# Graph convolution with two feature sets on one Trainium2 core: one more short turn at the start, sums on other tiles, later loads of x, and halves in the middle items

## The chip, the cores and the metric

The kernel runs on one core of one Trainium2 chip. The metric is the device time of one execution in microseconds. Before the change it is 392.65 us, the median of three runs (392.62 to 392.72).

## The reference

Both layers share the matrix, so the kernel treats x and spatial_x as one matrix of 256 columns:

```python
N, IN_DIM, HID = 4096, 128, 128
def _gcn_layer(x, adj, W, b):
    d_inv_sqrt = (jnp.sum(adj, axis=1) + 1e-09) ** (-0.5)
    msg = d_inv_sqrt[:, None] * adj * d_inv_sqrt[None, :] @ x
    return jax.nn.relu(msg @ W + b)
H_f = _gcn_layer(x, adj, W_f, b_f)
H_s = _gcn_layer(spatial_x, adj, W_s, b_s)
attn = jax.nn.sigmoid(jnp.concatenate([H_f, H_s], axis=1) @ W_att + b_att)
out = _layernorm(x + attn * H_f + (1.0 - attn) * H_s)
```

adj is 4096 x 4096 in float32, 64 MiB, and is read twice: once transposed for the product, once in natural order for the row sums.

## The kernel before, in words

The product A @ Y, where Y = D x (D is the row's inverse root), is cut into j-tiles (t, 32 tiles of 128 columns of adj) and row groups (g, 8 groups of 512 rows). A block is one t and one g, 128 x 512 numbers of the transposed matrix. Four blocks make an item, one transfer of 1 MiB, and `plan` lists the 64 items. A run is a row group with a list of tiles that are summed in one pair of PSUM banks (`pair`, four of them) before VectorE adds the pair into `acc` (an evacuation, two halves, `evacuate`). A turn is the set of four runs that take the pairs in their order; the groups 0 to 3 and the groups 4, 6, 5, 7 take turns. At the start of the program D is known for few tiles, so turns are short there; later a turn has four tiles: two old ones, whose blocks stand two by two in `column` items, and two fresh ones in `spread` items. The last eight tiles (item 48, FINAL, and on) go group by group.

Each item goes through the engines thus:

- SyncE issues the transfers in program order: `parts[k]` (pieces of natural rows for the row sums, up to 1 MiB), x, then item k into one of three `raw` buffers. It waits for VectorE's `low` of item k-3, and for GpSimd's sums of it.
- ScalarE makes Ah, `raw` rounded to fp32r (`high`), and sums the parts (`row_sum`, with an accumulator); `y_high` makes Yh.
- VectorE makes Al = raw - Ah (`low`), Yl (`y_low`), and evacuates. The order of these is written out in its loop over k.
- TensorE runs three products for each block and half of Y: Yh Ah, Yl Ah, Yh Al; an item has 24 matmuls of 512 columns. Up to item 21, `first_block` takes the first block in an order that needs Al and Yl late, and the two halves of Y end together.
- GpSimd makes D from the row sums (`degree`), and adds the blocks of row groups 6 and 7 for the j-tiles in SUMMED into S (`sum_block`), so that the last rows' sums need not be read in full. `collect`, on TensorE after item 42, turns S into eight columns; it waits for all sums and for the last evacuation of pair 3.

`pieces(k)` says in how many parts Ah and Al are made: blocks (0), (1), (2, 3) up to item 13, two halves up to item 21, and one piece after that. One constant, HALVED = 22, sets where the pieces end, where `sweeps` groups two blocks of one run, and where VectorE's order changes.

## Time and profile before

| what | value |
|---|---|
| median of the runs | 392.65 us |
| the profiled execution, its own time | 393.04 us |
| its span in the trace | 391.2 us |
| TensorE busy | 378.3 us, 97% |
| VectorE busy | 303.2 us, 77% |
| ScalarE busy | 285.6 us, 73% |
| GpSimd busy | 155.3 us, 40% |
| granted TensorE clock, mean | 0.994 of full |
| HBM read | 128.32 MB |

The span is the time between the first and the last record; the 1.8 us around it belong to the execution's own time. Busy time of TensorE is modelled from pipelined matmuls and overlaps, so the starts of its weight loads (PEld) are the better measure of its pace. A row of the timeline gives start and length, and in brackets how long the engine stood idle ahead of it and who released it. Two rows of a kind that follow each other are merged (x2).

### The profile page before, as it was taken

The page shows a single profiled execution, that of the slowest core. Times are in us where ns is not written, and L with a number is a line of the kernel's source. Part 1 is how long each engine was busy: PE and PEld are TensorE (multiplying, and loading weights), DVE is VectorE, ACT ScalarE, POOL GpSimd, SP SyncE. Part 2 cuts the span into 40 slices and gives each one's busy share as a digit, 9 for nine tenths or more (in the row PEclk, how much of TensorE's full clock was granted, in tenths as well). Part 3 has the DMA queues.
Part 4 walks back from the last instruction along what each step waited for, and adds up shares of the span by engine and source line. Part 5 has one row for each costly group of instructions (what it writes and reads, how often), then busy time and mean ns, then how long its engine had stood idle before and what let it go on. Part 6 is the DMA issues. An engine that isn't in the chain of part 4 may idle for free. (4 is left out here: it accounts for less than half of the span.)

```text
span 391.2 us, 5501 instructions
## 1 busy us (share of the span) xinstructions
PE 378.3 (97%) x1778; PEld 314.0 (80%) x1778; DVE 303.2 (77%) x443; ACT 285.6 (73%) x381; POOL 155.3 (40%) x204
## 2 busy tenths in 40 slices
PE   7889999999999999999999999999999999999992
PEld 7667778788888888788888888888788888888992
DVE  2789997999578975769578583928976796889795
ACT  3668788888877887878878887778742666687556
POOL 2332611571066402670058220010100417877795
PEclk9999999999999999999999999999999999999997
DMA  8999999999999999999999999999775534445002
GB/s 268 423 417 424 420 412 421 423 419 418 421 416 421 423 418 420 421 420 422 418 423 420 424 414 423 413 390 415 232 281 208 213 108 160 164 157 168 4 25 81
DMA packets 24556, 130.77 MB, mean 334 GB/s; under 512 B 2640, under 2 KB 7632, under 8 KB 10448
## 3 DMA queue, kind: packets, MB, share of 16 engines
q1 hardware_dynamic: 24528, 130.43, 83.2%
q8 instruction: 14, 0.23, 0.2%
q14 instruction: 14, 0.11, 0.1%
HBM read 128.32 MB, written 2.10 MB: 333 GB/s over the span
## 5 line engine op out<-in xcount | busy, mean ns | idle before, releaser
L533 DVE TENSOR_TENSOR Al<-raw,Ah 128x2048 fp32r<-128x2048 f32 (+2 forms) x101 | 162.0, 1620 | 40.3 <-ACT Ah L721 40.2
L408 PE MATMUL sums<-Ah,Yh 128*128 128x512 f32 (+1 forms) x484 | 186.9, 386 | 1.3 <-DVE Al L533 1.3
L409 PE MATMUL sums<-Ah,Yl 128*128 128x512 f32 (+1 forms) x484 | 185.1, 382 | 0.0
L410 PE MATMUL sums<-Al,Yh 128*128 128x512 f32 (+1 forms) x484 | 185.0, 382 | 0.0
L721 ACT ACTIVATE Ah<-raw 128x2048 fp32r<-128x2048 f32 (+2 forms) x101 | 127.1, 1283 | 48.9 <-DMA raw<-in_At 29.9
L731 ACT ACTIVATE nat<-nat 128x2048 f32<-128x2048 f32 (+1 forms) x54 | 100.1, 1855 | 20.0 <-DMA nat<-in_adj 19.3
L408 PEld LDWEIGHTS sums<-Ah,Yh 128*128 128x128 f32 x484 | 91.0, 188 | 22.5 <-DVE Al L533 4.8
L410 PEld LDWEIGHTS sums<-Al,Yh 128*128 128x128 f32 x484 | 91.0, 188 | 17.9
L409 PEld LDWEIGHTS sums<-Ah,Yl 128*128 128x128 f32 x484 | 91.0, 188 | 17.1
L553 DVE TENSOR_TENSOR acc<-sums,acc 128x512 f32<-128x512 f32 (+1 forms) x122 | 76.8, 673 | 28.8 <-PE sums L410 25.2
L871 POOL TENSOR_TENSOR S<-S,raw 128x512 f32<-128x512 f32 x40 | 62.4, 1559 | 32.2 <-DMA raw<-in_At 29.2
L829 POOL TENSOR_SCALAR dg<-rs 128x1 f32<-128x1 f32 x23 | 13.9, 603 | 112.4 <-ACT nat L731 112.3
L877 POOL TENSOR_TENSOR fin<-fin 128x128 f32<-128x128 f32 x31 | 15.2, 491 | 31.3 <-ACT fin L755 31.2
L878 POOL TENSOR_TENSOR xs<-xs,fin 128x128 f32<-128x128 f32 x31 | 22.2, 715 | 0.0
L764 ACT ACTIVATE fin<-xs,less 128x128 f32<-128x128 f32 x30 | 11.7, 390 | 14.1 <-POOL less L883 14.1
L542 DVE SCALAR_TENSOR_TENSOR Yl<-xs,D,Yh 128x256 fp32r<-128x256 f32 x32 | 20.8, 664 | 0.1
L748 ACT ACTIVATE Yh<-xs,D 128x256 fp32r<-128x256 f32 x32 | 15.4, 496 | 4.7 <-POOL D L832 2.4
L597 DVE SCALAR_TENSOR_TENSOR xs<-fin,att,xs 128x128 f32<-128x128 f32 x30 | 12.0, 414 | 7.8 <-POOL xs L878 7.6
L755 ACT ACTIVATE fin<-nat 128x256 f32<-128x256 f32 x32 | 11.8, 410 | 8.1 <-DVE nat L567 8.0
L441 PEld LDWEIGHTS sums<-Wfs,acc 128*128 128x128 f32 x128 | 15.6, 191 | 1.0 <-DVE acc L553 0.5
L441 PE MATMUL sums<-Wfs,acc 128*128 128x128 f32 x128 | 16.3, 276 | 0.1
L832 POOL TENSOR_TENSOR D<-dg,mhalf 128x1 f32<-128x1 f32 x23 | 15.0, 652 | 1.9
(56 smaller groups left out, 201.2 us busy)
## 6 DMA issues: line engine op xcount, KB each, us to landing
raw<-in_At SPq DMA_DIRECT2D x63, 1024.0 KB, 9.8
nat<-in_adj SPq DMA_DIRECT2D x47, 1024.0 KB, 12.0
nat<-in_adj SPq DMA_DIRECT2D x8, 768.0 KB, 9.6
xs<-in_xs SPq DMA_DIRECT2D x5, 512.0 KB, 11.1
out<-xs SPq DMA_DIRECT2D x15, 128.0 KB, 1.8
xs<-in_xs SPq DMA_DIRECT2D x5, 256.0 KB, 11.5
nat<-in_adj SPq DMA_DIRECT2D x2, 512.0 KB, 6.6
raw<-in_At SPq DMA_DIRECT2D x2, 512.0 KB, 8.5
```

The costliest lines, as they stand in the source:

```text
L408: pe.matmul(to, Yh[:, t % YRING, hs], high, start=first, stop=False)
L409: pe.matmul(to, Yl[:, t % YRING, hs], high, start=False, stop=False)
L410: mm = pe.matmul(to, Yh[:, t % YRING, hs], low, start=False, stop=last)
L441: return pe.matmul(sums[:, 3, bank, c + half * H:c + (half + 1) * H], acc[:, r // GT, half, q * P:(q + 1) * P], Wfs[:, half * H:(half + 1) ...
L533: dve.tensor_tensor(Al[:, k % SPLITS, a * IB:b * IB], raw[:, k % RAWS, a * IB:b * IB], Ah[:, k % SPLITS, a * IB:b * IB], ALU.subtract).the ...
L542: dve.scalar_tensor_tensor(out=Yl[:, r % YRING, :], in0=xs[:, r, :], scalar=D[:, r:r + 1], in1=Yh[:, r % YRING, :].bitcast(F32), op0=ALU.mult,
L553: dve.tensor_tensor(acc[:, g, half, a:b], sums[:, pair, half, 0:b - a], acc[:, g, half, a:b], ALU.add).then_inc(evac_ok, 1)
L721: act.activation(Ah[:, k % SPLITS, a * IB:b * IB], raw[:, k % RAWS, a * IB:b * IB], ACT.Copy).then_inc(high_ok, b - a)
L731: act.activation(nat[:, n % NATS, 0:width], nat[:, n % NATS, 0:width], ACT.Copy, accum_out=rs[:, r, h:h + 1]).then_inc(rs_act, 1)
L748: act.activation(Yh[:, r % YRING, :], xs[:, r, :], ACT.Copy, scale=D[:, r:r + 1]).then_inc(Yh_ok, 1)
L871: pool.tensor_tensor(S[:, g, :], S[:, g, :], raw[:, k % RAWS, j * IB:(j + 1) * IB], ALU.add).then_inc(block_sum_ok, 1)
L878: pool.tensor_tensor(xs[:, r, 0:F], xs[:, r, 0:F], f[:, H_S], ALU.add).then_inc(res_ok, 1)
```

## The change

- `plan` has one more short turn: tiles [3, 4], [4, 5] and [5, 6, 7] in place of [3, 4, 5]; the longer turns begin with tiles 6 and 7, and the sets of row groups swap.
- GpSimd sums tiles 2 to 21 in place of 0 to 19. The rest of each of the last rows is then two stretches of columns, and its load two transfers.
- Parts 10 and 11 go from item 9 to item 10, 12 and 13 one item later each.
- x of four tiles (`X_AFTER`) is issued one item ahead of its use, not four.
- HALVED becomes two constants: BY_BLOCK = 22, as before, for the order of blocks and of VectorE, and IN_PARTS = 50 for `pieces` and `first_block`, so items 22 to 49 come in halves.
- At items 47 and 48 VectorE's evacuations and Yl stand in another order, and the run of item 45 in pair 3 (LATE) is evacuated last of these.

```diff
-HALVED = 22
+BY_BLOCK = 22
+IN_PARTS = 50
...
-    for n, tiles in enumerate([[0], [0, 1], [1, 2], [2, 3], [3, 4, 5]]):
+    for n, tiles in enumerate([[0], [0, 1], [1, 2], [2, 3], [3, 4], [4, 5], [5, 6, 7]]):
         spread(add_runs(sets[n % 2], tiles, range(4)), tiles)
-    for n in range(3, FRONT // 2):
+    for n in range(4, FRONT // 2):
         old, fresh = [2 * n - 2, 2 * n - 1], [2 * n, 2 * n + 1]
-        new = add_runs(sets[n % 2], old + fresh, range(4))
+        new = add_runs(sets[(n + 1) % 2], old + fresh, range(4))
...
-    evac_order = sorted(range(len(runs)), key=lambda e: done_no[e, 0])
+    LATE = next(e for e in range(len(runs)) if end_item[e] == FINAL - 3 and runs[e][2] == 3)
+    evac_order = sorted(set(range(len(runs))) - {LATE}, key=lambda e: done_no[e, 0])
+    evac_order.insert(1 + max(evac_order.index(e) for e in evac_order if end_item[e] == FINAL - 1), LATE)
...
-    SUMMED = range(5 * GT)
-    PLAIN_FROM = len(SUMMED) * P
+    SUMMED = range(2, 22)
+    PLAIN = [(0, SUMMED[0] * P), ((SUMMED[-1] + 1) * P, N)]
+    PLAIN_COLS = sum(b - a for a, b in PLAIN)
...
-    parts[4], parts[6], parts[8], parts[9] = [4, 5], [6, 7], [8, 9], [10, 11]
-    for n in range(12, 30):
+    parts[4], parts[6], parts[8], parts[10] = [4, 5], [6, 7], [8, 9], [10, 11]
+    parts[11], parts[12], parts[13] = [12], [13], [14, 15]
+    for n in range(16, 30):
         parts[n - 2].append(n)
...
-    X_AFTER = {y_position(m * GT) - 4: m for m in range(3, G)}
+    X_AFTER = {y_position(m * GT) - 1: m for m in range(3, G)}
...
-            return [(0, 2), (2, GT)] if k < HALVED else [(0, GT)]
+            return [(0, 2), (2, GT)] if k < IN_PARTS else [(0, GT)]
...
-                    in_first = k < HALVED and j == 0
+                    in_first = k < IN_PARTS and j == 0
...
-                        if k in (FINAL - 1, FINAL):
-                            evacuate_new(ending[:1])
-                        for r in y_at[k]:
+                        if k == FINAL:
+                            evacuate_new(ended)
+                        if k != FINAL - 1:
+                            for r in y_at[k]:
+                                y_low(r)
+                    elif k == FINAL - 1:
+                        evacuate_new(ending[:1])
+                        for r in y_at[k][:2]:
+                            y_low(r)
+                    elif k == FINAL:
+                        for r in y_at[k - 1][2:]:
                             y_low(r)
...
-                if k < HALVED or k in (FINAL - 1, FINAL):
+                if k < BY_BLOCK:
                     evacuate_new(ending)
+                if k == FINAL:
+                    evacuate_new(ending + [LATE])
```

VectorE, items 8 to 10 before. Al is `low`, Yl `y_low`, acc an evacuation (one row for each half of a run), the first four rows are item 8, the next four item 9:

```order
L533 TENSOR_TENSOR Al<-raw,Ah 128x512
L542 SCALAR_TENSOR_TENSOR Yl<-xs,D,Yh 128x256
L533 TENSOR_TENSOR Al<-raw,Ah 128x512
L533 TENSOR_TENSOR Al<-raw,Ah 128x1024
L533 TENSOR_TENSOR Al<-raw,Ah 128x512
L542 SCALAR_TENSOR_TENSOR Yl<-xs,D,Yh 128x256
L533 TENSOR_TENSOR Al<-raw,Ah 128x512
L533 TENSOR_TENSOR Al<-raw,Ah 128x1024
L553 TENSOR_TENSOR acc<-sums,acc 128x512 x4
L533 TENSOR_TENSOR Al<-raw,Ah 128x512 x2
L533 TENSOR_TENSOR Al<-raw,Ah 128x1024
L553 TENSOR_TENSOR acc<-sums,acc 128x512 x4
```

The same place in the changed kernel, items 8 to 10:

```order
L541 TENSOR_TENSOR Al<-raw,Ah 128x512
L550 SCALAR_TENSOR_TENSOR Yl<-xs,D,Yh 128x256
L541 TENSOR_TENSOR Al<-raw,Ah 128x512
L541 TENSOR_TENSOR Al<-raw,Ah 128x1024
L561 TENSOR_TENSOR acc<-sums,acc 128x512 x4
L541 TENSOR_TENSOR Al<-raw,Ah 128x512 x2
L561 TENSOR_TENSOR acc<-sums,acc 128x512 x2
L541 TENSOR_TENSOR Al<-raw,Ah 128x1024
L561 TENSOR_TENSOR acc<-sums,acc 128x512 x2
L541 TENSOR_TENSOR Al<-raw,Ah 128x512
L550 SCALAR_TENSOR_TENSOR Yl<-xs,D,Yh 128x256
```

Eight evacuation halves now stand among the pieces of item 9, and item 9 has no Yl of its own; Yl of tile 5 has gone to item 10.

SyncE from x of tiles 4 and 5 on (the row with xs), before; raw is an item's transfer (here items 8, 9 and 10), nat a part:

```order
L368 DMA xs<-in_xs 128x512
L347 DMA raw<-in_At 128x2048
L357 DMA nat<-in_adj 128x2048 x2
L347 DMA raw<-in_At 128x2048
L357 DMA nat<-in_adj 128x2048
L347 DMA raw<-in_At 128x2048
```

In the changed kernel:

```order
L376 DMA xs<-in_xs 128x512
L353 DMA raw<-in_At 128x2048 x2
L363 DMA nat<-in_adj 128x2048 x2
L353 DMA raw<-in_At 128x2048
L363 DMA nat<-in_adj 128x2048
L353 DMA raw<-in_At 128x2048
```

Item 9 is issued right behind item 8, and two parts stand behind it.

VectorE from item 46 to item 48 before, beginning with the evacuation ahead of item 46:

```order
L553 TENSOR_TENSOR acc<-sums,acc 128x512 x2
L533 TENSOR_TENSOR Al<-raw,Ah 128x2048
L553 TENSOR_TENSOR acc<-sums,acc 128x512 x4
L533 TENSOR_TENSOR Al<-raw,Ah 128x2048
L553 TENSOR_TENSOR acc<-sums,acc 128x512 x2
L542 SCALAR_TENSOR_TENSOR Yl<-xs,D,Yh 128x256 x4
L553 TENSOR_TENSOR acc<-sums,acc 128x512 x4
```

In the changed kernel, up to the evacuations behind item 48:

```order
L561 TENSOR_TENSOR acc<-sums,acc 128x512 x2
L541 TENSOR_TENSOR Al<-raw,Ah 128x1024
L561 TENSOR_TENSOR acc<-sums,acc 128x512 x2
L541 TENSOR_TENSOR Al<-raw,Ah 128x1024
L561 TENSOR_TENSOR acc<-sums,acc 128x512 x2
L541 TENSOR_TENSOR Al<-raw,Ah 128x1024 x2
L561 TENSOR_TENSOR acc<-sums,acc 128x512 x2
L550 SCALAR_TENSOR_TENSOR Yl<-xs,D,Yh 128x256 x2
L541 TENSOR_TENSOR Al<-raw,Ah 128x1024
L561 TENSOR_TENSOR acc<-sums,acc 128x512 x2
L541 TENSOR_TENSOR Al<-raw,Ah 128x1024
L550 SCALAR_TENSOR_TENSOR Yl<-xs,D,Yh 128x256 x2
```

Between item 47 and the first piece of item 48 stand now one run and two Yl, where three runs and four Yl stood.

## Rows read from the trace of the kernel before

**Rows 1.** The page: engine busy us (share) and count; GB/s in 40 slices.
```profile
PE 378.3 (97%) x1778; PEld 314.0 (80%) x1778; DVE 303.2 (77%) x443; ACT 285.6 (73%) x381; POOL 155.3 (40%) x204
...
GB/s 268 423 417 424 420 412 421 423 419 418 421 416 421 423 418 420 421 420 422 418 423 420 424 414 423 413 390 415 232 281 208 213 108 160 164 157 168 4 25 81
```

**Rows 2.** Timeline, weight loads: start us, us, what, idle before and releaser.
```profile
11.72 0.30 PEld L424 LDWEIGHTS sums<-Ah,Yh 128*128 128x128 f32 x2 [1.28 <-ACT Ah L721]
...
26.13 0.30 PEld L432 LDWEIGHTS sums<-Ah,Yl 128*128 128x128 f32 x2 [1.12 <-DVE Yl L542]
...
42.36 0.19 PEld L424 LDWEIGHTS sums<-Ah,Yh 128*128 128x128 f32 x1
...
59.93 0.19 PEld L424 LDWEIGHTS sums<-Ah,Yh 128*128 128x128 f32 x1
...
65.37 0.19 PEld L424 LDWEIGHTS sums<-Ah,Yh 128*128 128x128 f32 x1
...
76.89 0.30 PEld L428 LDWEIGHTS sums<-Al,Yh 128*128 128x128 f32 x2 [0.23 <-DVE Al L533]
...
164.41 0.19 PEld L408 LDWEIGHTS sums<-Ah,Yh 128*128 128x128 f32 x1 [0.96 <-DVE Al L533]
...
280.86 0.19 PEld L408 LDWEIGHTS sums<-Ah,Yh 128*128 128x128 f32 x1 [0.43 <-issue]
```

**Rows 3.** Timeline, GpSimd: the adds into S of items 2 and 5.
```profile
22.82 2.98 POOL L871 TENSOR_TENSOR S<-S,raw 128x512 f32<-128x512 f32 x2
...
37.30 3.53 POOL L871 TENSOR_TENSOR S<-S,raw 128x512 f32<-128x512 f32 x2 [2.64 <-DMA raw<-in_At]
```

**Rows 4.** Timeline, VectorE, at items 2, 4, 8 and 48.
```profile
23.34 1.32 DVE L533 TENSOR_TENSOR Al<-raw,Ah 128x512 fp32r<-128x512 f32 x1 [1.11 <-ACT Ah L721]
...
24.58 1.50 DVE L542 SCALAR_TENSOR_TENSOR Yl<-xs,D,Yh 128x256 fp32r<-128x256 f32 x1
...
37.46 2.22 DVE L533 TENSOR_TENSOR Al<-raw,Ah 128x1024 fp32r<-128x1024 f32 x1 [0.18 <-ACT Ah L721]
...
58.36 0.68 DVE L533 TENSOR_TENSOR Al<-raw,Ah 128x512 fp32r<-128x512 f32 x1
...
58.96 0.47 DVE L542 SCALAR_TENSOR_TENSOR Yl<-xs,D,Yh 128x256 fp32r<-128x256 f32 x1
...
278.51 2.28 DVE L533 TENSOR_TENSOR Al<-raw,Ah 128x2048 fp32r<-128x2048 f32 x1
```

**Rows 5.** Windows, VectorE: stretch and its us, busy us, clock, DMA share, GB/s.
```profile
37.40:61.20 23.80, 23.71 (x31) 1.00 1.01 418
```

**Rows 6.** Timeline, ScalarE, where it waited for a landing or found it there.
```profile
34.82 0.63 ACT L721 ACTIVATE Ah<-raw 128x512 fp32r<-128x512 f32 x1 [1.20 <-DMA raw<-in_At]
...
57.78 1.92 ACT L731 ACTIVATE nat<-nat 128x2048 f32<-128x2048 f32 x1
...
62.81 0.63 ACT L721 ACTIVATE Ah<-raw 128x512 fp32r<-128x512 f32 x1 [0.55 <-DMA raw<-in_At]
...
159.52 1.92 ACT L721 ACTIVATE Ah<-raw 128x2048 fp32r<-128x2048 f32 x1 [0.57 <-DMA raw<-in_At]
```

**Rows 7.** Timeline, weight loads: starts of items 21 and 41, and `collect`.
```profile
130.85 0.19 PEld L424 LDWEIGHTS sums<-Ah,Yh 128*128 128x128 f32 x1
...
240.60 0.19 PEld L408 LDWEIGHTS sums<-Ah,Yh 128*128 128x128 f32 x1
...
251.58 0.54 PEld L475 LDWEIGHTS sums<-ones,S 128*128 128x128 f32 x4
```

**Rows 8.** Timeline, VectorE: two halves, evacuations behind items 21 and 41.
```profile
113.05 2.35 DVE L533 TENSOR_TENSOR Al<-raw,Ah 128x1024 fp32r<-128x1024 f32 x2
...
132.41 1.29 DVE L553 TENSOR_TENSOR acc<-sums,acc 128x512 f32<-128x512 f32 x2 [0.74 <-PE sums L432]
...
241.71 1.37 DVE L553 TENSOR_TENSOR acc<-sums,acc 128x512 f32<-128x512 f32 x2 [6.01 <-PE sums L410]
...
250.18 1.28 DVE L553 TENSOR_TENSOR acc<-sums,acc 128x512 f32<-128x512 f32 x2
```

More of the change, by code:

```diff
@@ L60, in plan @@
     tiles = [FRONT - 2, FRONT - 1]
-    column(add_runs(sets[0], tiles, [0, 1, 2, 0]), tiles)
+    column(add_runs(sets[1], tiles, [0, 1, 2, 0]), tiles)
     first = len(runs)
@@ L95, in sweeps @@
             n = i
-            while k >= HALVED and n < len(items[k]) and items[k][n][0] == items[k][i][0]:
+            while k >= BY_BLOCK and n < len(items[k]) and items[k][n][0] == items[k][i][0]:
                 n += 1
@@ L324, in nat_here @@
         def nat_here(eng, n):
-            eng.wait_ge(nat_in[n % NATS], 16 * (n // NATS + 1))
+            pieces_in = sum(len(PLAIN) if m >= 2 * FULL else 1 for m in range(n % NATS, n + 1, NATS))
+            eng.wait_ge(nat_in[n % NATS], 16 * pieces_in)
         def share_here(eng, i):
@@ L358, in load_part @@
                 else:
-                    sp.dma_start(nat[:, n % NATS, 0:N - PLAIN_FROM],
-                                 adj_r[r, :, PLAIN_FROM:N]).then_inc(nat_in[n % NATS], 16)
+                    c = 0
+                    for a, b in PLAIN:
+                        sp.dma_start(nat[:, n % NATS, c:c + b - a], adj_r[r, :, a:b]).then_inc(nat_in[n % NATS], 16)
+                        c += b - a
             def load_x(m):
@@ L658, in _ @@
                     if a == 0:
-                        if k >= HALVED and len(ending) == GT:
+                        if k >= BY_BLOCK and len(ending) == GT:
                             evacuate_new(ending[:2])
-                        if k in (FINAL - 1, FINAL):
-                            evacuate_new(ending[:1])
-                        for r in y_at[k]:
+                        if k == FINAL:
[9 more added lines that the diff above has]
+                        for r in y_at[k - 1][2:]:
                             y_low(r)
                     third_now = a == (1 if k < STEPWISE else 0) and items[k][0][0] != items[k][1][0]
-                    if k < HALVED and third_now:
+                    if k < BY_BLOCK and third_now:
                         evacuate_new(ending[:3])
-                if k < HALVED or k in (FINAL - 1, FINAL):
+                if k < BY_BLOCK:
                     evacuate_new(ending)
+                if k == FINAL:
+                    evacuate_new(ending + [LATE])
                 if k == COLLECT + 2:
@@ L682, in _ @@
                 if k < K - 1:
-                    evacuate_new(ended)
+                    evacuate_new([e for e in ended if e != LATE])
             evacuate(FIRST_LAST + TAIL - 1)
@@ L729, in row_sum @@
                 nat_here(act, n)
-                h, width = (n % 2, N // 2) if r < FULL else (0, N - PLAIN_FROM)
+                h, width = (n % 2, N // 2) if r < FULL else (0, PLAIN_COLS)
                 act.activation(nat[:, n % NATS, 0:width], nat[:, n % NATS, 0:width], ACT.Copy,
```

1 line of the change is left out of this document (removed).

## The prediction

> **What bounds the kernel now.** I read the page's busy shares first: TensorE is busy 97% of the span and moves from item to item at one pace, so the end is set by how often it waits. The slices show DMA at about 420 GB/s from the first tenth to two thirds of the span [rows 1], which is 1.05 MB in 2.5 us. A 1 MB transfer lands every 2.5 us whatever the engines do, so up to about 265 us landing times depend only on the order of issue. The weight-load timeline [rows 2] gives the pace: items 8 and 9 start at 59.93 and 65.37, 5.44 us for 24 matmuls. The same subtraction over the whole timeline (start of item k+1, less start of item k, less 5.44) leaves 6.2 us of waits, bar the small matmuls of `collect` and `weigh`: 4.7 us in items 0 to 7 (59.93 - 11.72 - 8 x 5.44), 0.20 in item 11 (the load at 76.89), 0.88 before item 27, 0.07 at 29 and 0.32 before item 48. Nothing after item 48 waits. The most that could be had is thus about 6 us, 1.6%.
>
> Where do the waits come from? Item 5 starts at 42.36 and item 8 at 59.93, so three items lost 17.57 - 16.32 = 1.25 us [rows 2]. In 37.4 to 61.2 VectorE is busy 23.71 of 23.80 us [rows 5]: in the short turns each item costs it about 2.4 us of `low`, half the time 2.4 of evacuations on top (1.28 for two halves one after the other [rows 8], four runs each turn's end), and what GpSimd takes. That part is seen at 22.82 [rows 3]: while the two adds into S run, a 512-wide `low` takes 1.32 us and a Yl 1.50, where without adds they take 0.68 and about 0.48 [rows 4]. An evacuation, with one operand in PSUM, shows no such growth. By the Trainium skill (SBUF — State Buffer, "SBUF: two separate sides") a GpSimd instruction and a VectorE one with two SBUF inputs lock each other out for a whole instruction; the trace agrees, each VectorE instruction being late by what was left of a 1.3 us add. Item 27 is another kind: its transfer lands at 159.52, then ScalarE takes 1.92 us for Ah [rows 6], VectorE makes Al, and TensorE starts only at 164.41, 4.9 us behind the landing [rows 2].
>
> **The change part by part.** *Sums gone from items 1 and 2.* Al and Yl are quicker by about 0.4 us in item 1 and 1.6 in item 2, and most of the wait of 1.12 at 26.13 [rows 2] goes, some 1.4 us in both items. I cost that at nothing. Item 4's transfer lands at 34.82 either way [rows 6]; its last `low` waits for ScalarE, not for VectorE's past, until 37.46 [rows 4], and meets the add of item 5 that starts at 37.30 [rows 3]. From there VectorE is never free until 61.2 [rows 5]. TensorE arrives earlier and waits longer; item 8 starts at 59.93 as now.
>
> *The extra short turn, and parts 10 and 11 later.* SyncE issues item 9 before two row-sum parts, so it lands where the part at 57.78 landed, not at 62.81 [rows 6]. Items 9 and 10 now carry two adds each, and item 9's run at 57.8, under `low` of item 8, which starts at 58.36 [rows 4]. The offsets of item 2 apply: from the first add's start, Al is ready after 1.84 us (22.82 to 24.66), Yl after 3.26 (26.08) [rows 3, 4]. That puts item 8's Yl at 61.06; TensorE wants it at 59.93 + 4 x 0.227 = 60.84, and the next block's Al at 61.72 against 61.55: item 8 loses 0.45. VectorE ends `low` of item 8 at 62.8, evacuates two runs (2.4), makes two blocks of item 9 (1.2), evacuates one (1.2) and is at 67.6 when it wants item 9's last half. TensorE wants that half at 65.8 + 2.73 = 68.5. Item 10's adds run from about 66.4 (its part is summed by 64.9, the degree takes 0.9). If VectorE gets in between the adds, the half is done at 68.8 (wait 0.35); if the second add goes first, at 70.1 (1.65). Between these ends I go by the like turn in before: items 5 to 7 lost 1.25 together [rows 2], of which I take 0.8 for item 9 after item 8's 0.45. **Term: +1.25.** The 0.20 of item 11, where evacuations and adds meet now, goes: **-0.20**. Items 11 to 13 carry no adds and the turn's evacuations end before TensorE wants the halves.
>
> *x later, and items 22 to 49 in halves.* x tiles 16 to 19 go behind item 29 instead of 26, so item 27 lands 1.25 us earlier (half a MB). With halves TensorE needs only the first half of Ah, about 1.05 us after landing (half of the 1.92 and a little). It would start at 159.5 - 1.25 + 1.1 = 159.4, where its own pace has it at 163.5: no wait, nor at 29. **Term: -0.95.** x must be there for `y_high`: each is issued ahead of the item that needs it, in queue order, so no wait comes. The price of halves: two 1024-wide `low` take 2.35 us, one 2048-wide 2.28 [rows 4, 8], 0.07 per item, hidden wherever VectorE has idle time. By the Trainium skill (VectorE: DVE Perf Modes, "The TRN2 errata") an SBUF instruction pays a fixed extra per instruction, an fp32 add of N being (N+151)/0.96 ns; that makes it 0.16 us, and the next term 0.77 in place of 0.59. The row decides.
>
> *first_block for items 22 to 49.* Now the two halves of an item's first block end together. In item 21 (start 130.85) the evacuation starts at 132.41, +1.56; in item 41 (start 240.60), still one half after the other, at 241.71, +1.11 [rows 7, 8]. So each turn's VectorE chain starts 0.45 later. That chain has slack where TensorE wants a half, but not at `collect`: VectorE works from 241.71 without a break to 251.46 (250.18 + 1.28), and `collect`, which waits for that last evacuation, starts at 251.58 [rows 7, 8]. With 0.45 and two splits (0.14) it starts at 252.17, and item 43 is behind it. **Term: +0.59.**
>
> *Other order at 47 and 48.* Before item 48, VectorE's `low` ended at 280.79 and TensorE waited until 280.86 [rows 2, 4], behind four Yl and six evacuation halves. The new order puts two Yl and three runs behind item 48's halves. Counted from item 45's start (S): first evacuation 1.56, item 48's first half at 12.9, TensorE at 16.3; no wait. Item 49's second half is done at 23.5, wanted at 23.8 (its third block comes after nine matmuls): 0.3 spare. **Term: -0.32.** The sums moved to items 40 and 41 fall where VectorE idles 6 us a turn [rows 8], the row sums' second DMA (1 KB rows) where transfers are ahead: nothing. Without that cover they would cost up to 1.7 us and some tenths.
>
> **Sum.** +1.25 - 0.20 - 0.95 + 0.59 - 0.32 = +0.37 us on the profiled execution's own 393.04, which stands 0.39 above the median of the runs (392.65). On the median: 393.0. It is no change: 0.2% is 0.79 us, about what a measurement of this kernel can tell.
>
> **The rivals.** *The early gain lives, faster.* If item 4 isn't held by its landing, or the adds of 9 and 10 slip between VectorE's instructions, 1.4 us of items 1 and 2 come through, or the 1.25 isn't lost: 391.5 to 391.8. For it: removal of adds is real at once in items 1 and 2. Against it: the landing at 34.82 and the unbroken VectorE stretch. Chance 0.27.
>
> *The new turn queues up, slower.* The second add goes first at item 9 (+0.85 over my term) and Yl or a block waits again, with the 0.3 spare of item 49 used up (+0.3): 393.8 to 394.3. It decides as soon as VectorE asks for item 9's last half after an add has started, at 67.6 against 67.7, so a tenth of a us turns it. Chance 0.23.
>
> *The wait at item 27 stays (the change doesn't do what it says)*: if the landing is not earlier, since the queue's order isn't its landing order, or halves are held by adds: +0.9, 393.9. Chance 0.05. My own case, within 392.2 to 393.7, has 0.45.
>
> **Numbers.** From these cases faster by over 0.2% (below 391.86) 0.24, within 0.44, slower 0.32. The range reaches from the early-gain case to the queueing one, 391.5 to 394.2; my case alone 392.2 to 393.7.
>
> **What would show it.** In the changed trace: the load that starts item 4's third block still near 39.7, and item 8 near 59.9; adds at 57.8 and 66 to 70 with Al and Yl near 1.4 us; item 12 starting about 1 us later than now (81.9); no load waiting near 164 or 280; `collect` 0.6 us after the last matmul of item 42. I am wrong if item 8 starts over 0.5 us earlier than now, if items 8 and 9 don't wait, or if a new wait stands after item 43.

## The result, and the profile after

The changed kernel takes 395.86 us (median of six executions, 394.89 to 397.99) against 392.69 for the kernel before (392.52 to 392.88): ratio 1.0091, 95% interval 1.0078 to 1.0104. It is slower, by 3.2 us in medians, where 0.4 was forecast. Two things stand out: the loss itself, and that the changed kernel's executions differ by 3 us where those of before agree within 0.4.

The page of the changed kernel's profiled execution (397.99 us, span 396.2), to be held against [rows 1]; the third line is the granted clock in 40 slices:

```profile
PE 379.7 (96%) x1778; PEld 314.7 (79%) x1778; DVE 318.2 (80%) x479; ACT 287.6 (73%) x409; POOL 161.4 (41%) x204
...
PEclk9899999999999999999999999999999999999997
...
GB/s 271 426 415 421 420 418 420 413 419 419 418 420 420 423 397 424 420 422 391 376 417 421 420 356 390 371 328 419 304 249 304 213 106 140 182 148 171 1 28 80
```

VectorE works 15.0 us more than before, of which 28 more `low` instructions explain only a part (below). The transfers, at 412 GB/s or more before from the 2nd to the 26th slice, now fall to 397, 391, 376, 356, 390, 371 and 328 in seven slices from the 15th to the 27th (the last of these was at 390 before). So the unbroken stream on which the forecast built ("landing times depend only on the order of issue") is broken. SyncE waits for `low` or for GpSimd's sums before it may issue into a buffer. Its own waits don't show the loss: those for `low` grow from 185.4 us in 52 to 224.0 in 58, but those for GpSimd's sums (49.0 to 27.5) and for the buffers of the row-sum parts (53.0 to 36.2) shrink, and the three together are 287 us in one and 288 in the other. They show only that `low` is now more often the last reader of a buffer.

The timeline of weight loads of the changed kernel, the loads that waited:

```profile
11.71 0.30 PEld L432 LDWEIGHTS sums<-Ah,Yh 128*128 128x128 f32 x2 [2.07 <-ACT Ah L739]
...
38.92 0.19 PEld L416 LDWEIGHTS sums<-Ah,Yh 128*128 128x128 f32 x1 [0.88 <-DVE Al L541]
...
60.39 0.30 PEld L440 LDWEIGHTS sums<-Ah,Yl 128*128 128x128 f32 x2 [0.40 <-DVE Yl L550]
60.99 0.19 PEld L416 LDWEIGHTS sums<-Ah,Yh 128*128 128x128 f32 x1 [0.30 <-DVE Al L541]
68.88 0.19 PEld L416 LDWEIGHTS sums<-Ah,Yh 128*128 128x128 f32 x1 [1.24 <-DVE Al L541]
145.99 0.19 PEld L416 LDWEIGHTS sums<-Ah,Yh 128*128 128x128 f32 x1 [1.04 <-issue]
184.48 0.19 PEld L416 LDWEIGHTS sums<-Ah,Yh 128*128 128x128 f32 x1 [0.54 <-DVE Al L541]
234.41 0.19 PEld L416 LDWEIGHTS sums<-Ah,Yh 128*128 128x128 f32 x1 [1.09 <-issue]
253.98 1.86 PEld L483 LDWEIGHTS sums<-ones,S 128*128 128x128 f32 x16 [0.65 <-issue]
283.23 0.30 PEld L432 LDWEIGHTS sums<-Ah,Yh 128*128 128x128 f32 x2 [0.38 <-DVE acc L561]
289.88 0.30 PEld L436 LDWEIGHTS sums<-Al,Yh 128*128 128x128 f32 x2 [0.87 <-DVE Al L541]
292.60 0.19 PEld L416 LDWEIGHTS sums<-Ah,Yh 128*128 128x128 f32 x1 [1.24 <-DVE Al L541]
375.81 1.86 PEld L449 LDWEIGHTS sums<-Wfs,acc 128*128 128x128 f32 x16 [0.77 <-DVE acc L561]
```

The same subtraction as in the forecast (start of the next item less start of this one less 5.44) gives what each item lost in before, in this execution, and in a second profile of the same kernel (experiment 5):

```
items     before   changed   changed, 2nd
0          0.37     1.89      1.92
1 to 3     2.60     0.00      0.23
4          0.47     0.79      0.99
5 to 7     1.25     1.21      1.21
8, 9       0.00     1.55      0.65
11         0.20     0.00      0.00
23         0.00     0.91      0.00
26 to 29   0.95     0.00      0.00
30         0.00     0.42      0.80
39         0.00     0.97      0.03
42         1.90     2.39      2.39   (holds the collect step)
47         0.39     0.34      0.03
49         0.00     1.87      1.82
62         2.20     3.03      3.00
sum       10.33    15.37     13.07
```

The differences, 5.0 and 2.7 us, are those of the executions' times within 0.1 (397.99 and 395.83 less 393.04). The forecast's terms at items 11, 26 to 29 and 42 are in the table at nearly their sizes, the one at items 8 and 9 at 1.55 and 0.65 for 1.25. What it did not have are items 23, 30, 39, 49 and 62, 5.0 and 3.5 us, all but the last in the stretch that was put in halves.

### The profile page after: what moved, and what is told of

Its sections match the earlier page's. It is cut to its first block and busy times, and to the rows that moved or that the text cites. A ratio compares the mean times of both kernels' runs of the same rounds, so it can differ in the third digit from the quotient of the medians.

```text
span 396.2 us, 5681 instructions
## 1 busy us (share of the span) xinstructions
PE 379.7 (96%) x1778; PEld 314.7 (79%) x1778; DVE 318.2 (80%) x479; ACT 287.6 (73%) x409; POOL 161.4 (41%) x204
## 5 line engine op out<-in xcount | busy, mean ns | idle before, releaser
L541 DVE TENSOR_TENSOR Al<-raw,Ah 128x1024 fp32r<-128x1024 f32 (+2 forms) x129 | 172.9, 1358 | 24.7 <-ACT Ah L739 24.2
L416 PE MATMUL sums<-Ah,Yh 128*128 128x512 f32 (+1 forms) x428 | 165.4, 386 | 3.7 <-DVE Al L541 2.2
L739 ACT ACTIVATE Ah<-raw 128x1024 fp32r<-128x1024 f32 (+2 forms) x129 | 130.9, 1045 | 48.4 <-DMA raw<-in_At 36.8
L417 PE MATMUL sums<-Ah,Yl 128*128 128x512 f32 (+1 forms) x428 | 163.8, 383 | 0.0
L418 PE MATMUL sums<-Al,Yh 128*128 128x512 f32 (+1 forms) x428 | 163.6, 382 | 0.0
L418 PEld LDWEIGHTS sums<-Al,Yh 128*128 128x128 f32 x428 | 80.7, 189 | 15.6
L417 PEld LDWEIGHTS sums<-Ah,Yl 128*128 128x128 f32 x428 | 80.8, 189 | 15.2
L432 PE MATMUL sums<-Ah,Yh 128*128 128x512 f32 x100 | 31.1, 392 | 1.9 <-ACT Ah L739 1.9
L436 PE MATMUL sums<-Al,Yh 128*128 128x512 f32 x100 | 31.2, 393 | 0.5 <-DVE Al L541 0.4
L440 PE MATMUL sums<-Ah,Yl 128*128 128x512 f32 x100 | 31.5, 396 | 0.0
L436 PEld LDWEIGHTS sums<-Al,Yh 128*128 128x128 f32 x100 | 18.6, 188 | 5.1 <-DVE Al L541 1.4
L440 PEld LDWEIGHTS sums<-Ah,Yl 128*128 128x128 f32 x100 | 18.9, 190 | 4.6 <-DVE Yl L550 0.8
```

Of the source, the lines that this page charges most:

```text
L416: pe.matmul(to, Yh[:, t % YRING, hs], high, start=first, stop=False)
L417: pe.matmul(to, Yl[:, t % YRING, hs], high, start=False, stop=False)
L418: mm = pe.matmul(to, Yh[:, t % YRING, hs], low, start=False, stop=last)
L432: pe.matmul(sums[:, pair, half, :], Yh[:, t % YRING, half * H:(half + 1) * H], high, start=first, stop=False)
L436: pe.matmul(sums[:, pair, half, :], Yh[:, t % YRING, half * H:(half + 1) * H], low, start=False, stop=False)
L440: mm = pe.matmul(sums[:, pair, half, :], Yl[:, t % YRING, half * H:(half + 1) * H], high, start=False, stop=last)
```

## The experiments

Eighteen runs; 5 and 13 repeat a kernel unchanged. "Changed" and "before" are the two kernels of this study; the kernel before ran beside each, at medians of 392.58 to 392.65. Times are medians; the ratios take in all executions, so where a few stand apart the two differ a little. Edits are shown in part; "..." stands for what is left out. Where it is said "whole", items 22 to 49 are taken in whole blocks as before.

**1. Old order at items 47 and 48.**

```
-    evac_order.insert(1 + max(...), LATE)
...
-                    elif k == FINAL - 1:
-                        evacuate_new(ending[:1])
...
+                        if k in (FINAL - 1, FINAL):
+                            evacuate_new(ending[:1])
...
```

> The changed kernel with the order of evacuations and Yl at items 47 and 48 as before, and nothing else undone. In the changed kernel's trace item 49 waits 0.87 us for its first Al and 1.24 us for its second half, behind six evacuation halves and four Yl on VectorE. If the new order costs that: the waits in item 49 shrink to under 0.5 us and the time falls by 1.5 to 2.2 us, to about 394. If item 49 is late because ScalarE or the transfers are late: the waits stay within 0.5 us of 2.1, time 395.5 or more.

Measured 396.18 us (396.20, 396.20, 396.16 and 394.44). The time is missed, the mechanism is not: item 49's 1.87 is gone, but in the profiled execution item 43 takes 1.55 us more, with no idle mark at all. The windows of this kernel show why (stretch, us, busy times, then granted clock, DMA share and GB/s):

```profile
254.20:259.20 5.00, 5.00 (x18) 3.96 (x17) 1.72 (x3) 4.21 (x6) 0.00 (x0) 0.66 1.02 375
```

TensorE is busy all the time, at a granted clock of 0.50 (1.2 GHz) for two thirds of it. The one execution at 394.44 fits the same kernel without that. Item 49's loss is gone although the transfers are late here too (ScalarE takes item 47 5.8 us before TensorE starts it, 4.3 and 4.6 us in the changed kernel's two traces), so the new order is needed for it.

**2. As 1, and whole blocks from item 22.**

```
-IN_PARTS = 50
+IN_PARTS = 22
```

> As the run with the old order, and items 22 to 49 in one piece again with no first_block there. The changed trace waits 0.91 at item 23, 0.42 at 30, 0.97 at 39 and 0.65 at collect. Theory: halves let each add into S slip in between two VectorE instructions and start the turn's chain 0.45 us later, so these waits go: 2.0 to 2.8 us less than the run with the old order, about 391.5 to 392.2. Rival: the waits come from where the adds now stand (items 22 to 25, 30 to 33, 38 to 41) and would be there with whole items too: under 0.8 us less.

Measured 393.24 (392.30 to 393.39, ten), ratio 1.0009 [1.0000, 1.0019]. The difference of 2.9 us is the first reading's, the time is not: it is 1.0 above the range. The halves cost 2.9 us beside the moved sums, and the spread goes with them. But this pair of traces does not put the 2.9 where the expectation had it. By the subtraction above, experiment 1 loses against this one 1.6 us at item 43 (the clock), 0.8 at item 62, 0.5 at item 42 and 0.8 in items 22 to 41; 0.8 goes the other way, at items 8, 9 and elsewhere. Against the one execution of 1 at 394.44 the halves cost 1.2.

**3. As 2, and x early again.**

```
-    X_AFTER = {y_position(m * GT) - 1: m for m in range(3, G)}
+    X_AFTER = {y_position(m * GT) - 4: m for m in range(3, G)}
```

> Only the short turn (with the parts moved) and the sums of tiles 2 to 21 are left of the change; x is early as before. If x one item ahead is what removes the wait at item 27 (0.88 us): this is 0.5 to 0.9 us slower than the run with x late and whole items. If x late does nothing or harms through late landings: equal or faster.

Measured 393.46 (392.69 to 394.30, eight). x later is worth 0.2 here, within the spread, not 0.95.

**4. The kernel before with the halves alone.**

```
-            return [(0, 2), (2, GT)] if k < HALVED else [(0, GT)]
+            return [(0, 2), (2, GT)] if k < IN_PARTS else [(0, GT)]     # 50, and so in_first
```

> The kernel before with items 22 to 49 in halves and first_block there, nothing else. Theory (halves make VectorE's chain longer where adds stand and at collect): item 27's wait of 0.88 goes, collect waits 0.6 more, and each turn with adds (26 to 29, 34 to 37) waits 0.5 to 1 at its second item: 393.5 to 395 us. Rival (halves only shorten the latency, the adds' places do the harm): 391.8 to 392.6.

Measured 392.71 (eight of ten at 392.58 to 393.37, two at 394.27 and 394.30), ratio 1.0012 [1.0001, 1.0023]. Alone the halves cost 0.1 in medians (0.4 in means, by the two slower executions), nearer the rival's range than the theory's. So it is not the halves by themselves, it is the halves with the rest: with the turn, the moved sums and x later, which 1 and 2 both have. No run adds the halves to one of these alone, so which of them is needed is not shown. The profiled execution is one of the two at 394.3, again with the clock down behind the collect step:

```profile
253.50:258.50 5.00, 5.00 (x16) 3.98 (x15) 2.86 (x4) 3.09 (x3) 0.00 (x0) 0.66 1.03 420
```

**5. The changed kernel again, unchanged.**

> The changed kernel once more, unchanged, for a second profile. The profile of the first shows new waits of TensorE at items 23, 30, 39, 42, 49 and 62 (0.9, 0.4, 1.0, 0.5, 1.9 and 0.8 us) and a granted clock of half from 12.9 to 16.2 us. That execution took 397.99 us, the median 395.86. Theory one (small differences of time decide whether GpSimd's adds come between two VectorE instructions): some of these waits are gone or elsewhere in the second profile, the sum of the new ones is 2 to 6 us, and it accounts for its time within 0.3 us. Theory two (the waits are fixed by the order of instructions): the same items wait within 0.2 us each, and what changes between executions is the stretch of half clock.

Measured 396.33 (395.83 to 396.84, four). Theory one holds in part: items 23 and 39 lose nothing this time, item 30 twice as much. But items 42, 49 and 62 lose the same in both, which it did not say. Another execution took 396.43 at a mean clock of 0.996, so the loss doesn't need a fallen clock.

**6. The changed kernel with GpSimd's adds of items 22 and later one column wide** (the column sums, and so the output, are incomplete for these blocks).

```
+                w = 1 if k >= 22 else IB
-                pool.tensor_tensor(S[:, g, :], S[:, g, :], raw[...],
+                pool.tensor_tensor(S[:, g, 0:w], S[:, g, 0:w], raw[...],
```

> The changed kernel, with GpSimd's column sums of items 22 and later over one column of a block in place of 512 (the sums, and so the output, are incomplete for these blocks). Theory one (the halves cost time because GpSimd's adds then come between the halves of Al and Yl and lengthen VectorE's chain before each new run): the waits at items 23, 30 and 39 go, 2.3 us, and the time falls to 393.0 to 394.0. Rival (the halves cost by themselves: one more instruction for ScalarE, VectorE and a later second half that holds back the next transfer): it stays above 395.0.

Measured 393.55 (six at 392.89 to 393.63, four at 394.64 to 394.93): 2.8 below the changed kernel beside it, as theory one has it. Items 23, 30 and 39 lose nothing, item 49 only 0.26. VectorE's timeline in front of item 23 shows what the adds do. The changed kernel, and under it its GpSimd:

```profile
136.49 2.19 DVE L541 TENSOR_TENSOR Al<-raw,Ah 128x1024 fp32r<-128x1024 f32 x1
138.60 1.28 DVE L561 TENSOR_TENSOR acc<-sums,acc 128x512 f32<-128x512 f32 x2
139.80 1.21 DVE L541 TENSOR_TENSOR Al<-raw,Ah 128x1024 fp32r<-128x1024 f32 x1
140.93 1.51 DVE L550 SCALAR_TENSOR_TENSOR Yl<-xs,D,Yh 128x256 fp32r<-128x256 f32 x1
142.37 2.31 DVE L541 TENSOR_TENSOR Al<-raw,Ah 128x1024 fp32r<-128x1024 f32 x1
...
136.31 3.53 POOL L889 TENSOR_TENSOR S<-S,raw 128x512 f32<-128x512 f32 x2
...
140.80 2.80 POOL L889 TENSOR_TENSOR S<-S,raw 128x512 f32<-128x512 f32 x2 [0.96 <-DMA raw<-in_At]
```

The kernel with thin adds at the same place:

```profile
136.06 1.22 DVE L541 TENSOR_TENSOR Al<-raw,Ah 128x1024 fp32r<-128x1024 f32 x1
137.19 1.28 DVE L561 TENSOR_TENSOR acc<-sums,acc 128x512 f32<-128x512 f32 x2
138.39 1.21 DVE L541 TENSOR_TENSOR Al<-raw,Ah 128x1024 fp32r<-128x1024 f32 x1
139.53 0.47 DVE L550 SCALAR_TENSOR_TENSOR Yl<-xs,D,Yh 128x256 fp32r<-128x256 f32 x1
139.92 1.21 DVE L541 TENSOR_TENSOR Al<-raw,Ah 128x1024 fp32r<-128x1024 f32 x1
```

A half of Al takes 1.22 us; with an add under it 2.19 and 2.31. Yl takes 0.47, with an add 1.51. These hits (instructions that start while an add runs and wait for it) cost 1.0 to 1.1 us whatever the length of what is hit; one that meets only the end of an add loses less (0.39 in experiment 11). The kernel of experiment 2 (whole) is hit there by adds at 137.41 and 141.88:

```profile
136.24 2.48 DVE L559 TENSOR_TENSOR acc<-sums,acc 128x512 f32<-128x512 f32 x4
139.01 3.29 DVE L539 TENSOR_TENSOR Al<-raw,Ah 128x2048 fp32r<-128x2048 f32 x1 [0.29 <-ACT Ah L727]
142.22 1.51 DVE L548 SCALAR_TENSOR_TENSOR Yl<-xs,D,Yh 128x256 fp32r<-128x256 f32 x1
```

The first pair falls mostly under four evacuations, which it does not delay (2.48, as without adds); Al is hit once, then Yl: two hits where the halves had three. Over the whole span, `low` is busy 172.9 us in 129 instructions in the changed kernel, 159.8 in 129 with thin adds, and 161.3 in 101 in experiment 2: the hits from item 22 on are some 13 us of the first. The transfers come back with the thin adds as well: the slices 15 to 27 are at 408 GB/s or more but for two (355 and 400). One thing this run does not separate: a thin add also lets go of its `raw` buffer sooner, so part of the 2.8 can be that and not the hits.

**7. The kernel before with x later and the moved sums.**

```
-    SUMMED = range(5 * GT)
+    SUMMED = range(2, 22)
-    X_AFTER = {y_position(m * GT) - 4: m for m in range(3, G)}
+    X_AFTER = {y_position(m * GT) - 1: m for m in range(3, G)}
```

> The kernel before with x three items later and the sums moved to j-tiles 2 to 21, without the short turn, the halves and the other order. If the short turn cost 1.25 to 1.55 us at items 8 and 9 and the waits at items 26 to 29 go with x, this takes 391.2 to 392.0. If what is lost at items 8 and 9 is given back by the transfers, as the whole-block form with the turn at 393.24 may suggest, it takes 392.3 to 393.0.

Measured 393.29: six at 391.64 to 393.32 and four at 394.62 to 395.10. Neither expectation holds. Without the short turn it is not faster but uneven, though nothing is in halves from item 22. Its trace (392.38) loses 2.40 at item 42, as the halves do.

**8. Experiment 1 with items 42 to 49 whole.**

```
-IN_PARTS = 50
+IN_PARTS = 42
```

> The changed kernel with the old order at items 47 and 48, and halves for items 22 to 41 alone (items 42 to 49 whole again). Its neighbour with halves to item 49 took 396.18. In that one's trace TensorE waits 0.64 us before the sums of the collect step, and the granted clock is half from 254.5 to 258.7 us, 1.55 us more for item 43. Theory one (that wait, of the first block in a half, lets the clock fall): without it the clock stays at 1.00 after item 42 and the time falls by 1.8 to 2.3, to 394.0 to 394.5. Rival (the clock falls for a wait elsewhere, or the loss lies in items 22 to 41): 395.5 to 396.3.

Measured 395.86 (394.87 to 396.26, four), inside the rival's range. The traced execution is the lowest (394.87), at a clock of 1.00 behind the collect step; items 23 and 30 lose 0.85 and 0.61, item 62 nothing more than before. Item 42 still loses 2.25 with whole blocks, so the wait that was to go is there, and this run tells little on the clock. That the three slower executions had the fallen clock is possible (one has a mean of 0.985), so the rival is likely rather than shown.

**9. The kernel before with x later alone.**

```
-    X_AFTER = {y_position(m * GT) - 4: m for m in range(3, G)}
+    X_AFTER = {y_position(m * GT) - 1: m for m in range(3, G)}
```

> The kernel before with nothing but x of four tiles three items later. The wait of 0.92 us at item 26 of the trace of before should go, and its 0.13 at item 28. If that comes through to the end, 391.6 to 392.1. Rival (the transfers are the bound up to there, and the time comes back as another wait for a block): 392.4 to 392.8.

Measured 392.62 (392.52 to 392.81, ten), ratio 1.0001 [0.9992, 1.0010]. The wait at item 26 is gone and comes back as 0.87 at item 19, where an add now meets a Yl (1.52 us in place of 0.47). The rival is right.

**10. The kernel before with the short turn alone.**

```
-    ... enumerate([[0], [0, 1], [1, 2], [2, 3], [3, 4, 5]]):
+    ... enumerate([[0], [0, 1], [1, 2], [2, 3], [3, 4], [4, 5], [5, 6, 7]]):
...     # and so the sets of row groups, and parts 10 to 15, as in the change
```

> The kernel before with the short turn and its row sums' places alone. The traces of the changed kernel show 0.40 us at item 8 and 1.15 or 0.29 at item 9 that the kernel before does not have, and 0.20 less at item 11. If these come through, 393.0 to 394.2. With the first two j-tiles' column sums left in, as here, GpSimd's adds come earlier, so if the adds under VectorE's chain set the wait, it may be less at item 9. Rival (the transfers are the bound up to item 40, so that an early wait is made good there): 392.4 to 392.9.

Measured 393.22 (392.81 to 393.77, ten), ratio 1.0017 [1.0007, 1.0026]. The turn costs 0.6: items 8 and 9 lose 0.37 and 0.27 in the trace, item 26 1.13 in place of 0.92, item 11 nothing in place of 0.20.

**11. The kernel before with the moved sums alone.**

```
-    SUMMED = range(5 * GT)
+    SUMMED = range(2, 22)
```

> The kernel before with nothing but GpSimd's column sums moved from j-tiles 0 to 19 to 2 to 21. With x later as well the times lay between 391.64 and 395.10, four of ten at 394.6 or more, three of these with a mean granted clock of 0.984 or 0.985. Theory one (two adds more under items 40 and 41 lengthen VectorE's chain there by 0.5 us, TensorE waits before the collect step, and in some executions the clock falls after that wait): times in two groups, 392.3 to 393.3 and 394.4 to 395.1, and a collect wait of 2.4 us. Rival (the sums cost nothing, x later does it): one group at 392.4 to 392.8.

Measured 394.68 (393.10, 394.65, 394.71, 394.73), ratio 1.0053 [1.0036, 1.0070]. The two groups are those of theory one, and the traced execution is in the lower. GpSimd's and VectorE's timelines before the collect step:

```profile
240.51 2.74 POOL L876 TENSOR_TENSOR S<-S,raw 128x512 f32<-128x512 f32 x2 [1.77 <-DMA raw<-in_At]
...
241.44 1.37 DVE L558 TENSOR_TENSOR acc<-sums,acc 128x512 f32<-128x512 f32 x2 [6.51 <-PE sums L415]
242.73 2.67 DVE L538 TENSOR_TENSOR Al<-raw,Ah 128x2048 fp32r<-128x2048 f32 x1
```

The last of the new adds ends under an Al, 0.39 longer than without (2.28), at the head of the chain that [rows 8] shows to have no slack; item 42 loses 2.26.

**12. Short turn and x later alone** (experiment 2 with the sums of before).

```
-    SUMMED = range(2, 22)
+    SUMMED = range(20)
```

> The changed kernel with whole blocks from item 22, the old order at items 47 and 48, and the column sums of before (j-tiles 0 to 19): the short turn and x later alone. Its neighbour with sums 2 to 21 took 393.24. If the moved sums are what costs 0.6 there, 391.6 to 392.6 and less spread. If the turn costs, 393.0 to 394.0.

Measured 392.57 (392.19 to 393.81, ten), ratio 1.0004 [0.9995, 1.0013]. Together they are worth nothing: what the turn costs, x gives back. The spread is not less (two of ten at 393.64 and 393.81). The moved sums make the 0.67 us to experiment 2.

**13. The moved sums alone again, unchanged.**

> The kernel with the moved column sums alone once more, unchanged: its times were 393.10 (the one with a trace), 394.65, 394.71 and 394.73 us. In the trace GpSimd's two new adds at 240.51 lie under VectorE's chain before the collect step, which waits 2.26 us in all (1.90 before), and the granted clock stays at 1.00 there. Theory (in the executions at 394.7 the clock falls after this wait): in a profiled execution near 394.7 the windows from 254 to 259 us show a granted clock near 0.5 for some 3.3 us, and item 43 is 1.5 us longer; one near 393.1 shows 1.00. Rival: a wait elsewhere makes up the 1.6 us.

Measured 393.97 (five at 393.12 to 393.38, five at 394.55 to 394.80). The two groups are there again, but the traced execution is again in the lower one, at a clock of 1.00 there, so it is not settled by its own trace.

**14. As 2, with sums of j-tiles 2 to 19.**

```
-    SUMMED = range(2, 22)
+    SUMMED = range(2, 20)
```

> Whole blocks from item 22, the old order at items 47 and 48, the short turn and x later, and GpSimd's column sums of j-tiles 2 to 19 alone (18 tiles in place of 20; ScalarE sums 256 columns more in each of 16 row tiles). If the early half of the moved sums gains and the late half is what costs, 391.9 to 392.5. If the early half gains nothing (its 0.3 us at item 8 lie within the spread of executions), 392.5 to 392.9.

Measured 392.99 (392.65 to 393.81, ten), ratio 1.0010 [1.0001, 1.0020], just above the second reading. It is 0.4 above experiment 12, with the sums of before, so to take the adds out of items 1 and 2 gains nothing that comes through.

**15. The changed kernel with thin adds in items 22 to 35 only** (the column sums of these blocks are incomplete).

```
+                w = 1 if 22 <= k < 36 else IB
```

> The changed kernel with GpSimd's adds of items 22 to 35 over one column of a block (the column sums of these blocks are incomplete), and those of items 36 and later whole. With all from item 22 on thin it took 393.55, unchanged 396.33. If the adds under the halves before items 23 and 30 carry the loss, and the lateness of the transfers that they leave behind makes the 1.8 us at item 49, 393.4 to 394.4. If the adds before item 39 and the collect step carry it, 395.3 to 396.3.

Measured 395.13 (394.21 to 395.56, four), between the two. In its trace (395.34) items 23, 30 and 39 lose nothing and item 49 0.73, but item 43 loses 1.53, again with the clock at half. Take that out and it is at 393.8, inside the first range; I count it as support for the first reading, not as proof.

**16. The other order alone on experiment 2** (items 47 to 49 in halves, 22 to 46 whole).

```
-IN_PARTS = 50
+IN_PARTS = [*range(22), 47, 48, 49]
-            ... if k < IN_PARTS else [(0, GT)]
+            ... if k in IN_PARTS else [(0, GT)]     # and so in_first
```

> The changed kernel with whole blocks in items 22 to 46 and halves in items 47 to 49 alone, the other order at items 47 and 48 kept. Its neighbour with the old order took 393.24. If the six evacuations in a row before item 49's Al cost by themselves, 394.4 to 395.2, with waits of 1.2 to 1.9 us at item 49. If they cost only where the transfers come late (item 49 waits 0.26 in the form with thin adds, 1.82 and 1.87 in the changed kernel), 392.9 to 393.6.

Measured 392.82 (391.85 to 393.04, ten): 0.42 below the old order (ratios 1.0001 and 1.0009, with intervals that overlap). Item 47's 0.39 is gone and item 49 loses nothing. Against the changed kernel this one differs in nothing but the halves of items 22 to 46, and it is 3.0 to 3.5 us faster.

**17. Short turn, x later and the other order; sums of before; halves only at 47 to 49** (experiment 16, and:)

```
-    SUMMED = range(2, 22)
+    SUMMED = range(20)
```

> What the runs leave of the change: the short turn, x later and the other order with halves in items 47 to 49, without the moved column sums and without halves in items 22 to 46. The short turn with x took 392.57, and the order was worth 0.39 at item 47 and 0.42 in time. If they add up, 391.9 to 392.4, faster than before by 0.1 per cent. If the early stretch takes it back, 392.4 to 392.9.

Measured 392.07 (391.86 to 392.41, eleven) against 392.58 (392.37 to 393.05): ratio 0.9985 [0.9976, 0.9994]. It beats both kernels, by 0.5 us the one before.

**18. The kernel before with the other order alone**, items 47 to 49 in halves (experiment 17, and:)

```
-    ... [2, 3], [3, 4], [4, 5], [5, 6, 7]]):
+    ... [2, 3], [3, 4, 5]]):
-    X_AFTER = {y_position(m * GT) - 1: m for m in range(3, G)}
+    X_AFTER = {y_position(m * GT) - 4: m for m in range(3, G)}
...     # and so the sets of row groups, and parts 10 to 15, as before
```

> The kernel before with the other order at items 47 and 48 and halves in items 47 to 49, nothing else. The wait of 0.39 at item 47 goes and none comes at item 49: 392.1 to 392.4. If a wait near item 49 takes its place, 392.5 to 393.2.

Measured 392.39 (392.09 to 392.70, eleven), ratio 0.9992 [0.9983, 1.0001], as the first reading has it, though the interval still touches 1; item 47 loses nothing, nor does item 49.

## Why the prediction was wrong

**The step that failed: "0.07 per item, hidden wherever VectorE has idle time".** It priced a split by two halves that stand back to back without an add. The add-free price is right (2.35 against 2.28). But a half is not only a shorter instruction, it is one more place for GpSimd to get in. GpSimd adds in pairs; behind a whole Al the second add of a pair waits (before: four adds take 9.44 us from 207.52), behind a half it gets in sooner and its next hit is on Al or Yl of the chain that a new run waits for. That is read from the timelines. That halves and adds carry the loss together is shown by the runs: without the halves of items 22 to 46 the changed kernel is 3.0 to 3.5 us faster (16), with thin adds 2.8 of its 3.7 (6), and the halves alone cost 0.1 (4). In the changed kernel's two traces, where the clock stays up, the hits make 2.3 and 0.8 us at items 23, 30 and 39 and, through late transfers, most of the 1.8 at item 49. In experiment 1 against 2 they are the smaller part: 0.8 of 2.9 in items 22 to 41, while 2.1 stand at items 42 and 43, behind the term of `collect` (below). The prediction had used this very lock for items 1, 2, 8 and 9 and left it out for items 22 to 41. By the Trainium skill (SBUF — State Buffer, "SBUF: two separate sides") whichever of the two instructions starts first holds the pair of ports to its end; the traces agree, with hits of 1.0 to 1.1 us, the same for instructions of 0.47, 1.22 and 2.28.

**"That chain has slack where TensorE wants a half"** failed with it: an undisturbed chain has it, a chain hit three times does not (1.04 at 145.99, 0.5 to 0.9 at item 30, 1.09 at 234.41).

**Other order, -0.32, "0.3 spare".** The size is right where transfers are on time: -0.42 (16 against 2), -0.50 (17 against 12), -0.19 (18), the first and the last within the spread. In the changed kernel it costs 1.8 at item 49 instead. Item 47's first half reaches ScalarE at 271.01 there, 4.6 us before TensorE starts the item; in experiment 16 at 268.04, 7.2 us before. ScalarE's timeline of the changed kernel's second profile and of experiment 16:

```profile
271.01 1.06 ACT L739 ACTIVATE Ah<-raw 128x1024 fp32r<-128x1024 f32 x1 [1.04 <-DMA raw<-in_At]
```

```profile
268.04 1.06 ACT L739 ACTIVATE Ah<-raw 128x1024 fp32r<-128x1024 f32 x1 [1.05 <-DMA raw<-in_At]
```

Then come six evacuations in a row and item 49's two halves, in VectorE's timeline of that second profile:

```profile
282.90 3.67 DVE L561 TENSOR_TENSOR acc<-sums,acc 128x512 f32<-128x512 f32 x6
286.49 1.21 DVE L541 TENSOR_TENSOR Al<-raw,Ah 128x1024 fp32r<-128x1024 f32 x1
287.62 1.67 DVE L550 SCALAR_TENSOR_TENSOR Yl<-xs,D,Yh 128x256 fp32r<-128x256 f32 x4
289.21 5.74 DVE L541 TENSOR_TENSOR Al<-raw,Ah 128x1024 fp32r<-128x1024 f32 x3
```

Al of item 49, wanted with its start at 286.54, is done at 287.7. In the seven traces with the new order the loss at item 49 goes with this lead of ScalarE: 4.3 us lose 1.87, 4.6 lose 1.82, 5.8 lose 0.73 (15), 6.3 lose 0.26 (6), 6.6 and more lose nothing (16, 17, 18). With the old order a lead of 5.8 loses nothing either (1, 8). The transfers are late since SyncE issues one only when the last reader of the buffer is done, and each hit on `low` delays that; with thin adds in items 22 to 35 (15) or from 22 on (6) they come earlier, as the leads show. So the rival's "0.3 spare used up" was the right place, at six times its price.

**x later and halves, -0.95.** The waits at items 26 to 29 did go (0.95 us in the table). As a gain it failed: alone it is 0.0 (9), beside the turn 0.6 (10 against 12), beside turn and sums 0.2 (3 against 2). A wait removed inside the stretch that the transfers and adds bound came back at another item.

**Short turn, +1.25.** The mechanism was as told, Yl at 60.39 and the block at 60.99 (0.40 and 0.30 of idle for 0.45), and one or the other order at item 9 (1.24 in one profile, near 0.3 in the next). In the thirteen traces with the turn item 8 loses 0.35 to 0.45 (0.85 in that of 6), and item 9 loses 0.22 to 0.31 in eight and 0.99 to 1.15 in five, where the two orders were put at 0.35 and 1.65. In time the turn alone costs 0.6, half of the term.

**Sums gone from items 1 and 2, nothing.** Right, in size and in reason. Item 8 starts at 59.08 to 59.79 in the thirteen traces without these adds and at 59.09 to 59.93 in the seven with them. Item 4's landing holds the stretch, as forecast: from ScalarE's first Ah of item 4, which waits for it, to the start of item 8 it is 25.08 to 25.16 us in all twenty traces. But the landing itself moves from execution to execution, 33.97 to 34.82, and the trace before had the latest of the twenty. So item 8 started 0.8 us earlier in the first trace of the changed kernel and 0.2 in the second, and the forecast's sign "item 8 starts over 0.5 us earlier than now" does not tell its cases apart.

**Sums moved to items 40 and 41, "nothing".** Wrong without the turn: 1.3 to 2.1 us (13, 11), where the prediction had named up to 1.7 for a lost cover. With the turn the last adds come at 228 to 238 instead and 0.67 remains (2 against 12).

**Collect, +0.59.** Measured +0.48 or +0.49 in all six traces with items 22 to 49 in halves. The wait was right; what follows it was not foreseen. The granted clock is at 0.50 for some 3.4 us behind it in the traces of 1, 4 and 15 (1.5 us each), and at 1.00 in both traces of the changed kernel and in 6, 7, 8, 11 and 13, with 2.25 to 2.45 us at item 42 too. None of the ten traces with 1.9 at item 42 shows it. Times of kernels 4, 6, 11 and 13 fall into two groups some 1.5 us apart (7: 2.0), those of 2, 9, 16, 17 and 18 do not, nor do 113 executions of the kernel before (392.25 to 393.05); 3, 10, 12 and 14, also with 1.9 at item 42, spread over 1.0 to 1.6 us without such groups. That this clock makes the upper groups is shown for 4 by its trace, and only likely for 6, 7, 11 and 13: of the twelve upper executions of 7, 11 and 13 six have a mean clock of 0.984 or 0.985, as the trace of 4 has (0.985), and none of the lower has one below 0.988. By the Trainium skill (TensorE: Matmul & The Clock Gate, "Part 1: The HAM clock gate") the monitor behind it runs free of the program, so one program can meet it in different phases; the traces, with and without the fall after one wait, agree.

**Sum.** In medians: turn and x 0.0, moved sums +0.7, halves +2.9 (of which the clock about 1.6, as the median of experiment 1 stands on executions like its trace), other order -0.3 or +0.15, by the first or the second median of the changed kernel. Forecast for the same four: +0.1, 0, +0.6, -0.3.

What stays open: why the 0.8 us at item 62 comes in some kernels. It is there in the changed kernel, 1, 5, 6 and 15 and not in the other fourteen, and no run was made for it. The traces show how it comes: by the same lock, at the last whole Al. The kernel before, and under it the changed kernel:

```profile
363.61 2.29 DVE L533 TENSOR_TENSOR Al<-raw,Ah 128x2048 fp32r<-128x2048 f32 x1
363.84 2.12 POOL L883 TENSOR_TENSOR less<-ysum,share 128x4 f32<-128x4 f32 x1 [0.64 <-DVE xs L597]
...
368.45 0.20 POOL L901 TENSOR_TENSOR less<-ysum,share 128x4 f32<-128x4 f32 x1 [0.64 <-DVE xs L605]
368.54 2.29 DVE L541 TENSOR_TENSOR Al<-raw,Ah 128x2048 fp32r<-128x2048 f32 x1 [0.23 <-issue]
...
372.66 0.68 DVE L584 SCALAR_TENSOR_TENSOR nat<-nat,watt 128x256 f32<-128x256 f32 x1
```

Before, GpSimd's small `less` (128x4, of the layer norm) comes 0.23 us behind the Al and takes 2.12; in the changed kernel it comes 0.09 us ahead and takes 0.20. GpSimd's later adds then start at 372.33, under four small products of VectorE, and three of these take 0.67 or 0.68 in place of 0.42. `less` is ahead in all five traces that lose 3.0 us at item 62 and behind in all fifteen that lose 2.2.

## What to carry to other kernels

Where two engines lock each other out for whole instructions, price a split by the number of times the other can get in, in the chain that somebody waits for, and not by the pair that stands alone in the trace. A transfer queue that is full in the trace before is full only while its buffers come free in time; after the change look at the GB/s slices first, since a wait removed in such a stretch comes back elsewhere. And a gain of tenths that leaves "0.3 spare" should be tried alone: here the order gave 0.2 to 0.5, and cost 1.8 next to a part that made its input late.

## What the runs showed of the hardware

- A wait of 0.65 us before sixteen small matmuls can be followed by 3.4 us at a granted clock of 0.50 (1, 4, 15), in some executions of a program and not in others; it adds 1.5 us to a busy TensorE that shows no idle mark. One has to see it in the loads' pace (0.43 in place of 0.23 us) or the windows.
- The same fall at 12.5 to 16.5 us (windows: 0.57 in the changed kernel, 1.00 in before) costs nothing at the end: item 0 loses 1.9 in place of 0.4 us and items 1 to 3 then 0 in place of 2.6, since all of it ends at the landing of item 4, and executions of the kernel before with a mean clock of 0.989 take 392.4 to 392.7 like those with 0.995 (0.989 and 0.995 are the means of the traces of 17, with this fall, and 18, without).
- An Al or Yl that meets a GpSimd add takes up to 1.1 us longer, the same for instructions of 0.47, 1.22 and 2.28 us and less where it meets only the add's end (0.39). An evacuation, with one operand in PSUM, takes no longer (0.67 to 0.69 us in the 25 of the changed kernel's trace that lie under an add). GpSimd pays too: its `less` takes 2.12 us behind an Al in place of 0.20.
